# State-space stage: another order of the calls on all five engines, and a wait for the bank of the chunk summary

## The chip, the cores and the metric

The program runs on one core of one Trainium2 chip. The metric is device time in microseconds (us) of one execution. Five engines work side by side, each through its own list of instructions in order: TensorE (PE, matmuls and transposes), VectorE (DVE), ScalarE (ACT), GpSimd (POOL) and SyncE (SP, which here only issues DMAs). They meet through semaphores alone.

## The reference

Four layers follow one another over 4096 tokens of 256 channels. Only the first is touched, a chunked state-space layer (8 heads of 64, state 64, inner width 512):

```python
zxbcdt = u @ W_in.T;  z, xBC, dt = split(zxbcdt);  dt = softplus(dt + dt_bias)
xBC = silu(causal_conv4(xBC) + conv_b);  x, Bm, Cm = split(xBC)
xs = x * dt;  A_cum = cumsum(-exp(A_log) * dt)                  # within a chunk
Y_diag = einsum('bcln,bcsn,bchls,bcshp->bclhp', Cr, Br, L, xs)   # within a chunk
states = einsum('bchl,bcln,bclhp->bchpn', decay_states, Br, xs)  # summary of a chunk
Y_off  = Cr @ carried_state * exp(A_cum)                         # carried into a chunk
y = (Y_diag + Y_off + x * D) * silu(z)
y = y * rsqrt(mean(y * y) + eps) * norm_w
x = layernorm(u + y @ W_out.T)
```

The chunks are joined by a running state `S`: each chunk decays it and adds its own summary. A coupling network, a selective scan and a quantised feed-forward layer follow, and are not changed.

## The kernel before

`first_layer` works on NB = 8 blocks of 512 tokens (index `b`), each of NC = 4 chunks of 128 (index `j`; `g = 4b + j`). Each engine has one function (`sync`, `tensor`, `vector`, `scalar`, `pool`) with small local functions, called below *calls*, each a few instructions with the semaphore waits that they need. The order of the calls is written out by hand in a loop over `it`, in which an engine works on several blocks at once: `it`, `post = it - 1`, `last = it - 2`, `old = it - 3`. Nothing else sets the order.

The calls, by engine:
- TensorE. `project_dt(b)` and `project(b, i)`, i = 1 to 9, make the input projection (i = 1 to 5 go through the convolution, 6 to 9 are z), six matmuls each, into banks `b_p0` and `b_p1`. `prepare(b, j)` transposes a chunk into banks `b_bc` and `b_xt`, and for j = 0 the block's dt as well. `carried(b, j)` multiplies the spread state `Sb` with `CE`, `within(b, j)` adds the chunk's own part (`M`, `xs`), both into bank `b_y`. `summary(b, j)` makes the chunk's summary in bank `b_new`. `project_out(b, j)` multiplies with `W_out` into bank `b_op`. `turn_out(b, j)` transposes a finished chunk, also into `b_new`.
- VectorE. `conv(b, i)` (three taps), `decays(b, j)` (two scans into `L`), `mask` (`M` from `L`), `inputs` (`xs`), `state` (`S = Sd + b_new`), `gate` (`zs = b_y * zs`), `mean_square` (`ssn` from `b_op`), `residual` (`r` from `b_op`, then statistics), `ramps`, `soft_err`.
- ScalarE. `evac_conv(b, i)` (two passes over a bank), `silu_conv`, `silu_z`, `direct(b, j)` (x * D into `b_y`, four instructions), `spread_S(b, j)` (`S` into `Sb`, two instructions), `square`, `evac_B`, `normalize`, `evac_out`, and the softplus in pieces (`row_parts`, `row_exp`, `row_log`, ...).
- GpSimd. `ramped` (`CE`), `decayed` (`xd`), `state` (`Sd`), `squares`, `root` (`rms`), `low_u` (`ul`), `soft_fix`, `norm`, `add_tokens`.
- SyncE. `load_uT`, `store_rows` and `load_rows` (decay rows out to memory and back, spread over 128 partitions), `copy_C`, `load_u`.

Dependences that matter below: `carried(b, j)` needs `direct(b, j)`, `spread_S` of the chunk ahead and `CE`, and `within(b, j)` stands behind it; `gate(b, j)` needs `within(b, j)`; `direct(b, j + 1)` needs `gate(b, j)`, since both use `b_y`. `project_out(b, j)` needs the bank that `residual` of the chunk ahead reads, and `mean_square(b, j)` needs `project_out(b, j)`. `decays(b, j)` overwrites `L`, which `decayed` of the chunk ahead (GpSimd) reads. `prepare(b, 0)` needs all of a block's `silu_conv` and the copy `C2`.

Of the kernel before, what the change touches and what calls it, by code (L numbers as in the profile page):

```python
# [14 lines left out]
NB = T // TB  # L15
# [28 lines left out]
def build(nc, d, out, scratch):  # L44
    with ExitStack() as ctx:
# [46 lines left out]
        def first_layer():  # L92
# [74 lines left out]
            def sync(e):  # L167
# [42 lines left out]
                e.dma_start(W_dt[:, :, :], rows(d["W_dtT"])).then_inc(ld_Wd, DMAS)  # L210
                load_uT(0)
                load_W(0)
# [6 lines left out]
                copy_C(0)  # L219
                load_rows(0, 0)  # L220
                load_rows(0, 1)
                load_nets()
                for it in range(NB + 2):
                    last, post = it - 2, it - 1
                    if 0 < last < NB:
                        load_rows(last, 1)
                    if live(last):
                        load_rows(last, 2)
                    if 1 < it < NB:
                        load_uT(it)  # L230
                    if live(last):
                        load_rows(last, 3)
                        load_u(last)
                    if 0 < post < NB:
                        store_rows(post)
                        copy_C(post)
                        load_rows(post, 0)
# [3 lines left out]
            def tensor(e):  # L241
# [113 lines left out]
                project(0, 8)  # L355
                prepare(0, 0)
                project(0, 9)
                for it in range(NB + 3):
                    old, last, post = it - 3, it - 2, it - 1
                    if 0 < post < NB:  # L360
                        prepare(post, 0)
                    if live(old):
                        turn_out(old, 0)
                    if live(last):
                        project_out(last, 2)
                    if 0 < it < NB:
                        project_dt(it)
                        project(it, 1)
                    if live(post):
                        carried(post, 0)  # L370
                    if live(old):
                        turn_out(old, 1)
                    if 0 < it < NB:
                        project(it, 2)
                    if live(post):
                        within(post, 0)
                    if live(old):
                        turn_out(old, 2)
                    if live(post):
                        prepare(post, 1)  # L380
                    if live(old):
                        turn_out(old, 3)
                    if 0 < it < NB:
                        project(it, 3)
                    if live(post):
                        summary(post, 0)
                    if 0 < it < NB:
                        project(it, 4)
                    if live(last):
                        project_out(last, 3)  # L390
                    if live(post):
                        carried(post, 1)
                        summary(post, 1)
                        within(post, 1)
                        prepare(post, 2)
                    if 0 < it < NB:
                        project(it, 5)
                    if live(post):
                        project_out(post, 0)
                        carried(post, 2)  # L400
                    if 0 < it < NB:
                        project(it, 6)
                    if live(post):
                        within(post, 2)
                        summary(post, 2)
                        prepare(post, 3)
                    if 0 < it < NB:
                        project(it, 7)
                    if live(post):
                        project_out(post, 1)  # L410
                    if 0 < it < NB:
                        project(it, 8)
                        project(it, 9)
                    if live(post):
                        carried(post, 3)
                        summary(post, 3)
                        within(post, 3)

            def scalar(e):
# [109 lines left out]
                split_W(0)  # L529
                row_parts(0)  # L530
                row_exp(0)
                row_log(0)
                split_W(1)
                halo(0)
                row_decay(0)
                evac_conv(0, 0)
                split_W(2)
                evac_conv(0, 1)
                evac_conv(0, 2)
                silu_conv(0, 0)  # L540
                evac_conv(0, 3)
                evac_conv(0, 4)
                split_u(1)
                silu_conv(0, 1)
                silu_conv(0, 2)
                silu_conv(0, 3)
                silu_conv(0, 4)
                silu_z(0, 0)
                silu_z(0, 1)
                evac_B(0, 0)  # L550
                silu_z(0, 2)
                direct(0, 0)
                silu_z(0, 3)
                for it in range(NB + 3):
                    old, last, post = it - 3, it - 2, it - 1
# [4 lines left out]
                    if live(last):  # L560
                        direct(last, 2)
                        evac_B(last, 2)
                    if 0 < post < NB:
                        evac_conv(post, 4)
                    if live(last):
                        square(last, 1)
                    if 1 < it < NB:
                        split_u(it)
                    if 0 < post < NB:
                        silu_conv(post, 0)  # L570
                        silu_conv(post, 1)
                    if live(last):
                        evac_B(last, 3)
                    if 0 < post < NB:
                        silu_z(post, 0)
                    if live(last):
                        square(last, 2)
                    if 0 < post < NB:
                        silu_conv(post, 2)
                        silu_z(post, 1)  # L580
                        silu_conv(post, 3)
                    if live(last):
                        direct(last, 3)
                        spread_S(last, 2)
                    if 0 < post < NB:
                        silu_conv(post, 4)
                        silu_z(post, 2)
                    if 0 < it < NB:
                        halo(it)
                    if live(old):  # L590
                        normalize(old)
                    if 0 <= last < NB - 1:
                        spread_S(last, 3)
                    if 0 < post < NB:
                        evac_B(post, 0)
                        silu_z(post, 3)
                        direct(post, 0)
                    if live(old):
                        evac_out(old, 0)
                    if live(last):  # L600
                        square(last, 3)
                    if 0 < it < NB:
                        row_parts(it)
                        evac_conv(it, 0)
                    if live(old):
                        evac_out(old, 1)
                    if 0 < it < NB:
                        evac_conv(it, 1)
                    if live(old):
                        evac_out(old, 2)  # L610
                    if 0 < it < NB:
                        row_exp(it)
                    if live(old):
                        evac_out(old, 3)
                    if live(post):
                        evac_B(post, 1)
                    if 0 < it < NB:
                        evac_conv(it, 2)
                        row_log(it)
                    if live(post):  # L620
                        direct(post, 1)
                        spread_S(post, 0)
                    if 0 < it < NB:
                        evac_conv(it, 3)
# [2103 lines left out]
```

## Time and profile before

| what | us |
|---|---|
| time, median of 3 runs | 1157.51 (1157.15 to 1159.94) |
| span of the profiled execution | 1157.9 |
| state-space stage in it | 0 to about 334 |
| steady blocks in it, by the transpose of dt in `prepare(b, 0)` | 37.95 each |
| TensorE / VectorE / ScalarE / GpSimd busy, share of the span | 90 / 81 / 75 / 65 % |

The span is the time from the first to the last instruction of one profiled execution, and is 0.4 us above the median. No time of its own beyond that span is given for that execution, so sums below are made against the span and carried over to the median. A busy TensorE in this profile is not one at its peak: the ends of matmuls are modelled and overlap, so that its pace is read from the distance between starts.

### The profile page before, as it was taken

How to read it: one execution, taken by the hardware profiler on the slowest of the kernel's cores; microseconds unless marked ns; L12 is line 12 of the kernel's file. 1: busy time of each engine (PE TensorE's matmuls, PEld its weight loads, DVE VectorE, ACT ScalarE, POOL GpSimd, SP SyncE). 2: the span in 40 equal slices, each digit the busy share in tenths (PEclk: the TensorE clock that was granted, in tenths of full speed). 3: DMA queues.
4: the chain of work that ended last, by engine and by line, in shares of the span. 5: the costliest groups of instructions: out<-in, count | busy, mean ns of one | idle time of the engine just before them, and what ended most of it. 6: DMA issues, size and time to landing. Idle time of an engine off the chain costs nothing. (4 is left out here: it accounts for less than half of the span.)

```text
span 1157.9 us, 17435 instructions
## 1 busy us (share of the span) xinstructions
PE 1041.0 (90%) x5234; PEld 702.9 (61%) x5234; DVE 940.3 (81%) x1313; ACT 871.2 (75%) x1681; POOL 750.9 (65%) x644
## 2 busy tenths in 40 slices
PE   6999999999879999995758699999999999987987
PEld 4777777777633344444436467566676756656576
DVE  7999999999824665453999899999999999999741
ACT  7768878877534455557777899899998989996733
POOL 3466656675722453343687988989798997979320
PEclk9999999999979999997778899999999999999899
DMA  6444343433231011114766555456555555745301
GB/s 191 131 126 133 115 128 106 132 117 113 83 136 48 1 37 55 37 55 130 208 155 139 132 152 128 138 148 153 139 143 159 145 138 146 152 135 130 73 1 37
DMA packets 93232, 133.83 MB, mean 116 GB/s; under 512 B 8786, under 2 KB 47698, under 8 KB 93140
## 3 DMA queue, kind: packets, MB, share of 16 engines
q1 hardware_dynamic: 93140, 132.73, 41.9%
q8 instruction: 42, 0.69, 0.2%
q14 instruction: 50, 0.41, 0.1%
HBM read 116.45 MB, written 14.16 MB: 113 GB/s over the span
## 5 line engine op out<-in xcount | busy, mean ns | idle before, releaser
L2228 DVE TENSOR_TENSOR_SCAN state<-bank_a,h,state 128x512 f32<-128x512 f32 x256 | 316.7, 1270 | 28.4 <-POOL state L2498 11.8
L2498 POOL TENSOR_TENSOR state<-uc,Bb 128x1024 f32<-128x1024 f32 x64 | 150.8, 2368 | 34.4 <-DVE prod L2234 24.8
L2498 POOL TENSOR_TENSOR state<-s,Bb 128x1024 f32<-128x1024 f32 x64 | 150.6, 2367 | 29.6 <-DVE prod L2234 21.1
L1663 PE MATMUL bank_y<-ident,prod 128*128 128x128 f32 x1024 | 140.6, 285 | 29.5 <-DVE prod L2234 29.5
L1663 PEld LDWEIGHTS bank_y<-ident,prod 128*128 128x128 f32 x1024 | 124.9, 148 | 68.6 <-DVE prod L2234 37.0
L2234 DVE TENSOR_TENSOR prod<-state,bank_c 128x1024 f32<-128x1024 f32 x128 | 154.2, 1204 | 5.0 <-ACT bank_c L1884 2.8
L1708 PE MATMUL bank_m<-w,f_h 128*128 128x256 f32 x448 | 106.0, 387 | 0.0
L40 PE MATMUL bank_m<-nT,w 128*128 128x512 f32 x224 | 103.8, 601 | 0.9 <-ACT nT L1962 0.9
L1879 ACT ACTIVATE bank_a<-s,A 128x512 f32<-128x512 f32 x128 | 86.2, 680 | 12.2 <-DVE state L2228 12.1
L1879 ACT ACTIVATE bank_a<-dtc,A 128x512 f32<-128x512 f32 x128 | 86.4, 681 | 10.5 <-DVE state L2228 10.3
L1708 PEld LDWEIGHTS bank_m<-w,f_h 128*128 128x128 f32 x448 | 83.3, 192 | 15.8 <-issue 5.8
L1884 ACT ACTIVATE bank_c<-Cb 128x512 f32<-128x512 f32 x128 | 75.3, 588 | 15.9 <-DVE prod L2234 15.8
L879 POOL TENSOR_TENSOR xd<-xs,L 128x512 f32<-128x512 f32 x32 | 34.0, 1062 | 76.4 <-DVE xs L660 76.4
L671 DVE TENSOR_TENSOR_SCAN L<-abc,zeros,b_id 128x512 f32<-128x512 f32 x64 | 78.3, 1265 | 5.2 <-POOL xd L879 4.2
L1318 DVE TENSOR_SCALAR cS<-cS,slope,shift 128x512 f32<-128x512 f32 x24 | 13.1, 546 | 67.5 <-ACT cS L1230 67.5
L40 PEld LDWEIGHTS bank_m<-nT,w 128*128 128x128 f32 x224 | 40.8, 193 | 39.0 <-issue 37.4
L334 PE MATMUL b_op<-W_out,zs 128*128 128x256 f32 x256 | 63.5, 391 | 0.0
L638 DVE SCALAR_TENSOR_TENSOR b_p<-raw,columns,b_p 128x512 f32<-128x512 f32 x72 | 54.3, 754 | 3.8 <-ACT b_p L465 2.2
L40 PE MATMUL c<-h,nets 128*128 128x512 f32 x96 | 46.7, 609 | 3.7 <-ACT h L1211 3.6
L40 PE MATMUL b_p<-uh,W_h 128*128 128x512 f32 x132 | 47.9, 444 | 2.0 <-DVE W_l L716 1.7
L334 PEld LDWEIGHTS b_op<-W_out,zs 128*128 128x128 f32 x256 | 46.6, 192 | 5.0
L1968 ACT ACTIVATE f_h<-bank_m,columns 128x512 f32<-128x512 f32 x56 | 38.0, 679 | 6.7 <-PE bank_m L40 5.9
(387 smaller groups left out, 2553.0 us busy)
## 6 DMA issues: line engine op xcount, KB each, us to landing
Bb<-CB_rows SPq DMA_DIRECT2D x128, 256.0 KB, 4.1
Cb<-CB_rows SPq DMA_DIRECT2D x128, 256.0 KB, 4.7
abc<-decays SPq DMA_DIRECT2D x32, 512.0 KB, 4.5
Ebc<-ramps SPq DMA_DIRECT2D x64, 128.0 KB, 3.1
uT<-in_uT SPq DMA_DIRECT2D x8, 512.0 KB, 4.4
u<-in_u SPq DMA_DIRECT2D x8, 512.0 KB, 4.1
x_tokens<-x2s SPq DMA_DIRECT2D x8, 512.0 KB, 2.9
x_rows<-x1T SPq DMA_DIRECT2D x8, 512.0 KB, 2.7
```

Source lines behind the costliest of these rows:

```text
L40: i = e.matmul(out, w, x, start=(n == 0), stop=(n == len(pairs) - 1))
L334: i = e.matmul(b_op[:, 0:DM], zs[b % 2][:, m, ts], W_out[:, m, :], start=(m == 0), stop=(m == MD - 1))
L638: e.scalar_tensor_tensor(to, raw[:, m, t:t + TB], cw[:, m, t:t + 1], acc[:, :], ALU.mult, ALU.add).then_inc(v_conv, 1)
L671: e.tensor_tensor_scan(L[:, hs, :].rearrange("p h t -> p (h t)"), abc[g % 2][:, hs, :].rearrange("p h t -> p (h t)"), b_id[:, :], zeros[:, ...
L1663: i = e.matmul(p_y[c // 2][:, at:at + P], prod[n % 2][:, k, c * CH:(c + 1) * CH], ident[:, :], start=False, stop=(n == NS - 1), is_transpo ...
L1708: i = e.matmul(to, f_h[:, k, c * CH:(c + 1) * CH], w2[:, k, :], start=False, stop=(c % 2 == 1 and k == KF - 1))
L1879: e.activation(p_a[k][:, :], dtc[b % 2][:, k, :], ACT.Exp, scale=A[:, k, n:n + 1]).then_inc(a_a, 1)
L1884: e.activation(p_c[:, :], Cb[n % 4][:, :], ACT.Copy).then_inc(a_c, 1)
L1968: e.activation(f_h[:, m, :], pair[m % 2][:, :], ACT.Identity, bias=b1[:, m:m + 1]).then_inc(a_up, 1)
L2228: e.tensor_tensor_scan(s[:, k, :], p_a[k][:, :], s[:, k, :], h0[:, n, k:k + 1], ALU.mult, ALU.add).then_inc(v_s, 1)
L2234: e.tensor_tensor(prod[n % 2][:, :, :], state[(NS * b + n) % 3][:, :, :], both(p_c[:, :]), ALU.mult).then_inc(v_g, 1)
L2498: e.tensor_tensor(state[at % 3][:, :, :], uc[b % 2][:, :, :], both(Bb[n % 4][:, :]), ALU.mult).then_inc(p_b, 1)
```

## The change

All calls stay, with the same shapes and data. Their order is written anew on TensorE, ScalarE, VectorE and SyncE; on GpSimd only the first `low_u` moves, ahead of `scale_W_out`. One wait is added, in `summary`: `after(e, v_S, g)`, that is, `state` of the chunk ahead has read `b_new`. Before, `carried` of the same chunk, which waits for `spread_S` of the chunk ahead, stood ahead of `summary` and implied it.

```diff
@@ summary(b, j), TensorE
                     e.wait_ge(a_Bt, g + 1)
                     e.wait_ge(p_xd, g + 1)
+                    after(e, v_S, g)
                     after(e, a_tx, NC * (b - 1))
@@ SyncE, in the loop
                     if 0 < last < NB:
+                        store_rows(last)
+                        load_rows(last, 0)
                         load_rows(last, 1)
+                    if 1 < cur < NB:
+                        load_uT(cur)
                     if live(last):
                         load_rows(last, 2)
-                    if 1 < it < NB:
-                        load_uT(it)
-                    if live(last):
                         load_rows(last, 3)
                         load_u(last)
                     if 0 < post < NB:
-                        store_rows(post)
                         copy_C(post)
-                        load_rows(post, 0)
@@ TensorE, ahead of the loop
                 project(0, 8)
+                project(0, 9)
                 prepare(0, 0)
-                project(0, 9)
@@ TensorE, last part of the loop
+                    if 0 < cur < NB:
+                        project(cur, 7)
+                        project(cur, 8)
+                        project(cur, 9)
+                    if live(post):
+                        summary(post, 3)
+                    if 0 < cur < NB:
+                        prepare(cur, 0)
                     if live(post):
                         carried(post, 3)
-                        summary(post, 3)
+                    if 0 < nxt < NB:
+                        project_dt(nxt)
+                    if live(post):
                         within(post, 3)
+                    if live(last):
+                        turn_out(last, 0)
+                    if live(post):
+                        project_out(post, 2)
@@ VectorE, from the loop
                     if live(last):
-                        residual(last, 0)
+                        decays(last, 3)
+                        inputs(last, 3)
+                        state(last, 2)
                         gate(last, 2)
-                        decays(last, 3)
-                        state(last, 2)
-                        inputs(last, 3)
                         mean_square(last, 1)
@@ ScalarE, last part of the loop
                     if live(post):
                         square(post, 0)
+                    if 0 < cur < NB:
+                        row_plus_one(cur)
+                    if live(post):
+                        evac_B(post, 2)
+                        direct(post, 2)
```

On TensorE, at the end of a block's chunks (block 0's chunk 3, with projections of block 1), the order before was this; `b_y<-CE,Sb` is `carried`, `b_y<-M,xs` `within`, `b_new` `summary`, `b_bc` and `b_xt` `prepare` of the next block, `b_op` `project_out` of chunk 2, `b_p<-uT` `project_dt`.

```order
L301 MATMUL b_y<-CE,Sb 128x128 x4
L322 MATMUL b_new<-xd,Bt 64x256 x2
L310 MATMUL b_y<-M,xs 64x128 x8
L285 MATMUL b_bc<-ident,r_dt 128x128
L286 MATMUL b_bc<-ident,xf 128x128
L287 MATMUL b_bc<-C,xf 128x128
L291 MATMUL b_xt<-ident,xf 128x128 x4
L332 MATMUL b_op<-ones,sq 128x1
L334 MATMUL b_op<-W_out,zs 128x256 x4
L40 MATMUL b_p<-uT,W_dt 32x128 x8
```

And now:

```order
L322 MATMUL b_new<-xd,Bt 64x256 x2
L284 MATMUL b_bc<-ident,r_dt 128x128
L285 MATMUL b_bc<-ident,xf 128x128
L286 MATMUL b_bc<-C,xf 128x128
L290 MATMUL b_xt<-ident,xf 128x128 x4
L300 MATMUL b_y<-CE,Sb 128x128 x4
L40 MATMUL b_p<-uT,W_dt 32x128 x8
L309 MATMUL b_y<-M,xs 64x128 x8
L332 MATMUL b_op<-ones,sq 128x1
L334 MATMUL b_op<-W_out,zs 128x256 x4
```

`summary` and `prepare(b + 1, 0)` now stand ahead of `carried(b, 3)`, and `project_dt` ahead of `within(b, 3)`.

On VectorE, the stretch from the `gate` of chunk 2 to the `decays` of the next block (`zs` is `gate`, `L` `decays`, `S` `state`, `xs` `inputs`, `ssn` `mean_square`, `M` `mask`) was this:

```order
L694 TENSOR_TENSOR zs<-b_y,zs 128x4x128
L671 SCALAR_TENSOR_TENSOR L<-abc,zeros,b_id 128x512 x2
L687 TENSOR_TENSOR S<-Sd,b_new 128x256
L660 TENSOR_TENSOR xs<-b_xt,dtT 128x512
L700 TENSOR_SCALAR ssn<-b_op 128x1
L680 TENSOR_TENSOR M<-L,b_bc 128x1024
L671 SCALAR_TENSOR_TENSOR L<-abc,zeros,b_id 128x512 x2
```

And now:

```order
L673 SCALAR_TENSOR_TENSOR L<-abc,zeros,b_id 128x512 x2
L662 TENSOR_TENSOR xs<-b_xt,dtT 128x512
L689 TENSOR_TENSOR S<-Sd,b_new 128x256
L696 TENSOR_TENSOR zs<-b_y,zs 128x4x128
L702 TENSOR_SCALAR ssn<-b_op 128x1
L682 TENSOR_TENSOR M<-L,b_bc 128x1024
L673 SCALAR_TENSOR_TENSOR L<-abc,zeros,b_id 128x512 x2
```

The `gate` of chunk 2 has gone behind `decays`, `inputs` and `state`, and `inputs` ahead of `state`.

On ScalarE, from the `square` of chunk 0 on (`Sb` is `spread_S`, `b_y<-xf` `direct`, `r_da` `row_decay`, `Bt` `evac_B`), the order was this:

```order
L504 ACTIVATE sq<-zs 128x512
L488 ACTIVATE Sb<-S 64x4x64
L489 ACTIVATE Sb<-S 64x4x64
L453 ACTIVATE r_da<-r_dt,negA 128x128
L497 ACTIVATE b_y<-xf,columns 128x128 x4
L482 ACTIVATE Bt<-b_bc 128x64
```

And now:

```order
L505 ACTIVATE sq<-zs 128x512
L447 ACTIVATE r_vd<-r_va 128x128
L483 ACTIVATE Bt<-b_bc 128x64
L498 ACTIVATE b_y<-xf,columns 128x128 x4
L489 ACTIVATE Sb<-S 64x4x64
L490 ACTIVATE Sb<-S 64x4x64
L454 ACTIVATE r_da<-r_dt,negA 128x128
```

`direct` of chunk 2 now stands ahead of `spread_S` of chunk 1, instead of behind it.

## Rows read from the trace of the kernel before

**Rows 1.** Busy time of each engine in one period: us, then PE, PEld, DVE, ACT, POOL, PEclk, DMA
```profile
137.90:175.87 37.97, 37.85 (x262) 29.45 (x261) 36.05 (x60) 30.95 (x71) 25.61 (x33) 1.00 0.40 122
```

**Rows 2.** Waits of VectorE, 45 to 290 us: total, times, longest
```profile
DVE L L671 <- POOL xd L879: 4.0, 6, 0.7
```

**Rows 3.** Timeline of VectorE in one period: start, length, instruction
```profile
133.49 0.69 DVE L660 TENSOR_TENSOR xs<-b_xt,dtT 128x512 f32<-128x512 f32 x1
...
141.70 0.15 DVE L700 TENSOR_SCALAR ssn<-b_op 128x1 f32<-128x1 f32 x1
...
142.52 2.45 DVE L671 TENSOR_TENSOR_SCAN L<-abc,zeros,b_id 128x512 f32<-128x512 f32 x2 [0.68 <-POOL xd L879]
...
158.06 0.41 DVE L687 TENSOR_TENSOR S<-Sd,b_new 128x256 f32<-128x256 f32 x1
...
159.57 0.69 DVE L694 TENSOR_TENSOR zs<-b_y,zs 128x512 f32<-128x512 f32 x1
```

**Rows 4.** Timeline of GpSimd in the same period
```profile
141.36 1.07 POOL L879 TENSOR_TENSOR xd<-xs,L 128x512 f32<-128x512 f32 x1
```

**Rows 5.** Timeline of TensorE over one period
```profile
137.85 0.33 PE L285 MATMUL b_bc<-ident,r_dt 128*128 128x128 f32 x1
...
141.99 0.73 PE L40 MATMUL b_p<-uh,W_h 128*128 128x512 f32 x2
...
156.93 0.33 PE L286 MATMUL b_bc<-ident,xf 128*128 128x128 f32 x1
...
158.02 0.71 PE L40 MATMUL b_p<-uh,W_h 128*128 128x512 f32 x2
...
161.59 1.16 PE L301 MATMUL b_y<-CE,Sb 128*128 128x128 f32 x8
...
162.56 0.73 PE L40 MATMUL b_p<-uh,W_h 128*128 128x512 f32 x2
...
164.28 1.09 PE L310 MATMUL b_y<-M,xs 128*64 128x128 f32 x16
...
165.74 0.33 PE L286 MATMUL b_bc<-ident,xf 128*128 128x128 f32 x1
...
167.12 0.72 PE L40 MATMUL b_p<-uh,W_h 128*128 128x512 f32 x2
...
171.95 0.63 PE L40 MATMUL b_p<-uh,W_h 128*128 128x512 f32 x2
...
173.36 1.05 PE L301 MATMUL b_y<-CE,Sb 128*128 128x128 f32 x8
...
175.80 0.33 PE L285 MATMUL b_bc<-ident,r_dt 128*128 128x128 f32 x1
```

**Rows 6.** Timeline of ScalarE, in a period and in the tail
```profile
138.72 0.41 ACT L489 ACTIVATE Sb<-S 64x256 f32<-64x256 f32 x1
...
160.30 1.25 ACT L497 ACTIVATE b_y<-xf,columns 128x128 f32<-128x128 f32 x4 [0.41 <-DVE zs L694]
...
300.54 0.41 ACT L489 ACTIVATE Sb<-S 64x256 f32<-64x256 f32 x1
...
311.58 1.23 ACT L497 ACTIVATE b_y<-xf,columns 128x128 f32<-128x128 f32 x4
```

**Rows 7.** Timeline of TensorE at the start and in the tail
```profile
25.83 0.69 PE L291 MATMUL b_xt<-ident,xf 128*128 128x128 f32 x4 [3.25 <-ACT xf L469]
...
26.25 1.14 PE L40 MATMUL b_op<-uh,W_h 128*128 128x512 f32 x2
...
301.20 1.13 PE L301 MATMUL b_y<-CE,Sb 128*128 128x128 f32 x8 [0.53 <-ACT Sb L489]
...
314.90 1.13 PE L301 MATMUL b_y<-CE,Sb 128*128 128x128 f32 x8 [1.86 <-POOL CE L870]
```

**Rows 8.** Timeline of VectorE at the start and in the tail
```profile
33.04 1.54 DVE L638 SCALAR_TENSOR_TENSOR b_p<-raw,columns,b_p 128x512 f32<-128x512 f32 x2 [1.21 <-ACT b_p L465]
...
310.32 0.69 DVE L694 TENSOR_TENSOR zs<-b_y,zs 128x512 f32<-128x512 f32 x1
```

More of the change, by code:

```diff
@@ L392, in tensor @@
                         carried(post, 1)
-                        summary(post, 1)
                         within(post, 1)
-                        prepare(post, 2)
-                    if 0 < it < NB:
-                        project(it, 5)
+                        project_out(post, 0)
+                    if 0 < cur < NB:
+                        project(cur, 5)
                     if live(post):
-                        project_out(post, 0)
                         carried(post, 2)
-                    if 0 < it < NB:
-                        project(it, 6)
+                        summary(post, 2)
@@ L403, in tensor @@
+                    if 0 < cur < NB:
+                        project(cur, 6)
                     if live(post):
+                        prepare(post, 3)
                         within(post, 2)
[L405 to L408, printed above, removed]
+                        project_out(post, 1)
+                    if 0 < cur < NB:
+                        project(cur, 7)
+                        project(cur, 8)
+                        project(cur, 9)
@@ L576, in scalar @@
[L576 to L589, printed above, removed]
@@ L590, in scalar @@
                     if live(old):
                         normalize(old)
+                    if 1 < cur < NB:
+                        split_u(cur)
+                    if 0 < post < NB:
+                        silu_z(post, 1)
+                        silu_conv(post, 4)
+                    if live(last):
+                        spread_S(last, 2)
+                        square(last, 2)
+                        direct(last, 3)
+                    if 0 < post < NB:
+                        evac_B(post, 0)
+                        silu_z(post, 2)
@@ L613, in scalar @@
+                    if 0 < cur < NB:
+                        evac_conv(cur, 1)
+                        silu_conv(cur, 0)
                     if live(old):
                         evac_out(old, 3)
[L615 to L619, printed above, removed]
+                    if 0 < cur < NB:
+                        row_exp(cur)
+                        evac_conv(cur, 2)
@@ L765, in vector @@
                 for it in range(NB + 2):
-                    last, post = it - 2, it - 1
+                    last, post, cur = it - 2, it - 1, it
+                    if live(last):
+                        state(last, 1)
+                        inputs(last, 2)
                     if 0 < post < NB:
@@ L788, in vector @@
                         residual(last, 1)
+                    if live(post):
+                        inputs(post, 0)
+                    if live(last):
                         gate(last, 3)
                     if live(post):
-                        inputs(post, 0)
                         mask(post, 0)
```

152 lines of the change are left out of this document (70 added, 82 removed).

## Prediction

> **What bounds the kernel now.** I read the windows of single periods first, then the waits of VectorE, then the timelines of the engines side by side. In a steady block TensorE and VectorE both count as full: 37.85 and 36.05 us busy of 37.97, at the full clock (PEclk 1.00), where ScalarE has 30.95 and GpSimd 25.61 [rows 1]. The busy sum of TensorE flatters it, since ends overlap, so VectorE's waits decide. They are all of one kind: six times 0.6 to 0.7 us, 4.0 us together, `decays` for `xd` on GpSimd [rows 2]. One period from one dt transpose to the next is 175.80 - 137.85 = 37.95 us [rows 5]; without its wait of 0.68 [rows 3] VectorE would need 37.27. That is the floor of any order, and six periods at it would give back 4.0 us, or 0.35%. The rest of what an order can change lies at the two ends: 1.21 us for which VectorE waits for the first `evac_conv` of block 1 [rows 8], and the tail behind the last block, where TensorE waits 1.86 us for `CE` [rows 7]. Everything from about 334 us on runs the same instructions. A measurement of this kernel tells from no change what is beyond about 0.3%, 3.5 us.
>
> **Part 1, the wait that goes.** Before, `inputs(b, 3)` starts on VectorE at 133.49, the `decays` that waits at 142.52: 9.03 us, of which 0.68 waiting, so 8.35 of work [rows 3]. GpSimd fills these 9.03 us with a chain that starts from this `inputs` and ends with `decayed(b + 1, 0)`, 141.36 + 1.07 = 142.43 [rows 4], 0.09 ahead of the `decays`. Now `state(b, 2)` and `gate(b, 2)` stand between the two on VectorE: 0.41 and 0.69 long [rows 3], less some 0.1 by which each overlaps the next, 0.9 together. VectorE reaches `decays` after 8.35 + 0.9 = 9.25, behind GpSimd's 9.03. GpSimd's order is unchanged there, so this wait goes, with 0.2 us to spare: worth 0.68 a period by itself.
>
> **Part 2, the wait that may come instead.** `project_out(b, 2)` moved to the end of TensorE's iteration, behind `summary(b, 3)`, `prepare(b + 1, 0)`, `carried(b, 3)`, `project_dt` and `within(b, 3)`, and `mean_square(b, 2)`, which reads it, stands right ahead of the `decays` of part 1. And ScalarE now does `direct(b, 2)` ahead of `spread_S(b, 1)`. That closes a loop through three engines, which I price once round:
> - VectorE from `mean_square(b, 2)` to `gate(b + 1, 1)`: 159.57 - 141.70 = 17.87, less the wait 0.68, less `state(b + 1, 1)`, which now comes after the gate, 0.32: 16.87 [rows 3].
> - gate start to `direct` start: 160.30 - 159.57 = 0.73; `direct` itself 1.25; `spread_S` behind it, two times 0.41, 0.82 [rows 3, 6].
> - `spread_S` end (300.54 + 0.41 = 300.95) to `carried` start (301.20): 0.25 [rows 6, 7].
> - TensorE from `carried(b, 2)` to the end of `project_out(b, 2)`. The same 16 calls stand in the trace in two pieces, 161.59 to 175.80 (14.21) and 137.85 to 141.99 (4.14), 18.35 together [rows 5]. Two calls in it hold waits: `project(b, 6)` takes 164.28 - 162.56 = 1.72 where `project(b, 9)` takes 173.36 - 171.95 = 1.41, and `prepare(b, 3)` takes 167.12 - 165.74 = 1.38 where `prepare(b, 2)` takes 158.02 - 156.93 = 1.09 [rows 5]. Less 0.31 and 0.29: 17.75.
> - the last matmul's end to `mean_square`, 0.1 as an estimate from releases in the trace (a gate that ends at 160.26 and the `direct` at 160.30).
>
> Sum: 16.87 + 0.73 + 1.25 + 0.82 + 0.25 + 17.75 + 0.10 = 37.77 us a round. A round is a period, so the period can't fall to 37.27; the wait of 0.68 turns into one of about 0.5 at `mean_square(b, 2)`, for TensorE. Gain 37.95 - 37.77 = 0.18, in six periods 1.1 us. The uncertain term is TensorE's 17.75. Where calls meet in other pairs, loads of weights are hidden better or worse. Bounds: not less than VectorE's floor (gain 4.0), and, if each of the four projections in it takes the 1.72 of the slowest in the period and nothing is subtracted for `prepare`, 17.75 + 4 x 0.31 + 0.29 = 19.28, 39.3 a round, a loss of 8.1. I take 37.77, since these are the durations of the same calls, with only the two clear waits taken out.
>
> **Part 3, the other moves.** The wait for `v_S` in `summary(b, 1)` costs nothing: `state(b, 0)` is now followed on VectorE by `mean_square(b - 1, 3)` and `conv(b + 1, 2)`, and TensorE has `project_out(b - 1, 3)` and `project(b + 1, 4)` ahead of this `summary`. Were that cover gone, `prepare(b, 2)`, `carried(b, 1)` and `within(b, 1)` would queue behind it and `gate(b, 1)` would wait for them; `carried(b, 1)` needs `spread_S` of the same `state` anyhow, so that at most the `summary` and `prepare` in front of it, about 1.6 us, would move into the path. `silu_conv(b, 0)` early on ScalarE, ahead of the exponential, adds no table load, as the z activations ahead of it use the same table; it waits for `conv(b, 0)`, and `evac_conv(b, 2)` behind it is wanted by VectorE only after `inputs`, `conv(b, 1)`, `gate`, `mask` and `state`. On SyncE `copy_C` is ahead of `store_rows` and `load_uT(b + 2)` ahead of `load_rows(b, 2)`; the only releaser of VectorE's waits in steady blocks is `xd`, never a DMA [rows 2], and each of these moves by one or two calls of a few us a period at most, so nothing for them.
>
> **Part 4, the start.** Two opposite things. `project(0, 9)` is now ahead of `prepare(0, 0)`. Before, TensorE idled 3.25 us in the middle of `prepare(0, 0)` and then ran that projection at the lower level of its clock, two matmuls in 1.14 us where 0.72 is usual [rows 5, 7]. Now it is out of the way of `project_dt(1)`, and VectorE's 1.21 us before `conv(1, 0)` [rows 8] shrink. Against this, uT(0) is loaded behind W(0), the first weights are split only after the logarithm, and `silu_conv(0, 0)`, from which `C2` is copied, comes behind `evac_conv(0, 4)`, so `prepare(0, 0)` starts later. Bounds: the whole 1.21 gained, or about 1 lost, by the projection (1.4) and split (1.05) that moved. I take 0.5 gained. By the Trainium skill, "TensorE: Matmul & The Clock Gate", What's actually happening, the array's default is the throttled state, and only activity releases it; the slow projection behind the gap agrees. By that rule the gap now meets `prepare(0, 0)` and `project_dt(1)` instead, half a microsecond of the gain would go, and the sum would end at 1156.7.
>
> **Part 5, the tail.** In the last block `gate(7, 2)`, before at 310.32 [rows 8], comes behind `decays`, `inputs` and `state`, 2.45 + 0.69 + 0.41 less overlaps, 3.3 us later [rows 3]; its `residual` ahead comes about 0.6 earlier, because `mask` now covers the root. So the gate is near 313.0, ScalarE squares (0.6) and then does `direct(7, 3)` (1.23 [rows 6]), and `carried(7, 3)` starts near 315.6 instead of 314.90 [rows 7]; but `summary(7, 3)`, 0.5, is no longer between it and `within(7, 3)`. Net 0.2 to 0.4 lost; I take 0.1 more for the round of part 2 that the last periods carry in, less what `mean_square(6, 3)` gives back, and put 0.3 lost in all (bounds 0.5 gained, 1.0 lost).
>
> **Sum.** -1.1 - 0.5 + 0.3 = -1.3 us on a span of 1157.9, which is 0.4 above the median of 1157.51: 1156.6 for the span, 1156.2 for the median.
>
> **Rivals.**
> - The loop is quicker than priced and VectorE runs at its floor. For it: TensorE's calls overlap in places, and part 1's slack is real. Against it: the 16 calls are priced from the trace, and 17.75 would have to be 17.25. Gain 4.0 + 1.2 at the start - 0.2: 1152.5. It counts as faster from a round below 37.5 together with 0.5 to 1 at the start. Chance 0.28.
> - The loop is slower, TensorE becoming the bound, since `direct(b, 2)` ahead of `spread_S(b, 1)` holds `carried(b, 2)` in every block. For it: a projection can take 1.72. Against: VectorE's mask ends just there. It decides from 37.95 + 3.7 / 6 = 38.6 a round; at 38.7 the loss is 4.5, less 0.2 at the ends: 1161.8. Chance 0.10.
> - The start or the tail misses by more than its bounds while the periods stay as forecast: 1154 to 1159, either side. Chance 0.05.
> - The forecast, a wait traded for a shorter one: 1156.2, by itself 1154.2 to 1158.3. Chance 0.57.
>
> The range leaves out the far part of the first two rivals: 1152.0 to 1160.5. Faster gets the first and half of the third rounded down, 0.30; slower the second and the rest, 0.13; same 0.57.
>
> **What would show it.** Right: the wait of `decays` for `xd` is gone from VectorE's list, and one of `mean_square`'s lines for `b_op` of about 0.5 us stands in its place, six or seven times; dt transposes 37.8 apart; `conv(1, 0)` near 32.5; the last `gate` about 0.3 later relative to the last period. Wrong: dt transposes 37.3 apart (first rival), or 38.6 and more with waits of TensorE for `Sb` (second); waits of VectorE with a DMA or ScalarE's `b_p` as releaser, which part 3 excludes, would break the argument itself.

## The result, and the profile after

| | before | changed |
|---|---|---|
| median, us | 1157.94 (1157.15 to 1160.08, 6 runs) | 1162.2 (1161.11 to 1163.79, 6 runs) |
| span of the profiled execution | 1157.9 | 1162.0 |
| last transpose of the stage (`x1T`) on ScalarE | 333.48 | 337.64 |
| one steady period | 37.95 | 38.95 |

The ratio is 1.0033, 95% interval 1.0022 to 1.0045: slower by 4.3 us, where 1.3 us faster was forecast, and 1.7 us above the range. All of it arises in the first layer, whose last `x1T` is 4.16 later.

To find the stretch, I take `soft_err`, which VectorE does once a block. From block 1 to block 7 it starts at 44.83 and 271.75 before, at 44.68 and 276.27 now. So the start gives 0.15, the six periods between take 4.67 more (231.59 for 226.92), and from there to the last `x1T` it is 61.37 for 61.73, 0.36 less: 4.16. The period is the whole question. Behind the last `x1T` every kernel runs the same instructions, and the profiled executions of this document take between 822.7 and 826.6 us for them. A difference of 1 or 2 us between the times of two kernels can thus lie there, and what an edit does to the loop is read from the period.

Windows of the changed kernel, one period (columns as in [rows 1]):

```profile
137.64:176.59 38.95, 38.27 (x262) 29.22 (x260) 36.80 (x59) 30.61 (x71) 25.57 (x33) 1.00 0.42 119
```

VectorE is busy 0.75 us more than in [rows 1] with the same calls, and TensorE 0.42, both at the full clock (1.00). What VectorE waits for, 45 to 290 us (total, times, longest):

```profile
DVE ssn L702 <- PE b_op L334: 2.8, 6, 0.5
DVE zs L696 <- PE b_y L309: 2.2, 6, 0.5
```

and TensorE in the same stretch:

```profile
PE b_y L300 <- ACT Sb L490: 3.5, 6, 0.6
PE b_p L40 <- DVE xf L640: 0.2, 1, 0.2
```

The wait for `xd` of [rows 2] is gone, and `mean_square` waits for `b_op` in its place, six times about half a microsecond: both as forecast. Besides, `gate` waits for `b_y`, and TensorE waits for `Sb`. Now the round of part 2, on VectorE:

```profile
143.96 0.16 DVE L702 TENSOR_SCALAR ssn<-b_op 128x1 f32<-128x1 f32 x1 [0.49 <-PE b_op L334]
...
159.43 0.78 DVE L644 SCALAR_TENSOR_TENSOR r_vd<-r_vd,r_va 128x128 f32<-128x128 f32 x1
...
161.31 0.69 DVE L696 TENSOR_TENSOR zs<-b_y,zs 128x512 f32<-128x512 f32 x1
```

on ScalarE:

```profile
156.14 0.60 ACT L464 ACTIVATE raw<-b_p 128x512 f32<-128x512 f32 x1 [1.19 <-PE b_p L40]
156.77 0.75 ACT L466 ACTIVATE b_p<-b_p,columns 128x512 f32<-128x512 f32 x1
157.45 0.40 ACT L489 ACTIVATE Sb<-S 64x256 f32<-64x256 f32 x1
157.86 0.41 ACT L490 ACTIVATE Sb<-S 64x256 f32<-64x256 f32 x1
...
158.52 0.61 ACT L505 ACTIVATE sq<-zs 128x512 f32<-128x512 f32 x1
...
162.03 1.25 ACT L498 ACTIVATE b_y<-xf,columns 128x128 f32<-128x128 f32 x4 [2.60 <-DVE zs L696]
163.22 0.40 ACT L489 ACTIVATE Sb<-S 64x256 f32<-64x256 f32 x1
163.63 0.42 ACT L490 ACTIVATE Sb<-S 64x256 f32<-64x256 f32 x1
```

on TensorE, to the end of `project_out(b, 2)`:

```profile
158.53 1.13 PE L300 MATMUL b_y<-CE,Sb 128*128 128x128 f32 x8 [0.58 <-ACT Sb L490]
...
164.31 1.13 PE L300 MATMUL b_y<-CE,Sb 128*128 128x128 f32 x8
165.37 0.65 PE L322 MATMUL b_new<-xd,Bt 128*64 128x256 f32 x4
165.95 0.73 PE L40 MATMUL b_p<-uh,W_h 128*128 128x512 f32 x2
...
167.44 0.27 PE L285 MATMUL b_bc<-ident,xf 128*128 128x128 f32 x1
...
168.65 1.09 PE L309 MATMUL b_y<-M,xs 128*64 128x128 f32 x16
...
180.75 0.28 PE L332 MATMUL b_op<-ones,sq 128*128 128x1 f32 x2
...
182.70 0.38 PE L344 MATMUL b_new<-ident,r 128*128 128x128 f32 x2
```

and on GpSimd, beside VectorE's 159.43:

```profile
159.33 0.72 POOL L901 TENSOR_TENSOR sq<-sq 128x256 f32<-128x256 f32 x1 [3.09 <-ACT sq L505]
```

The round closes exactly: `mean_square` to `gate` 161.31 - 143.96 = 17.35 (forecast 16.87), to `direct` 0.72 (0.73), to `carried` 164.31 - 162.03 = 2.28 (2.32), and `carried` to the next `mean_square`, 182.90, 18.59 (17.85): 38.94, the period to within the rounding of the rows. Two of its terms are off, by 0.48 and 0.74.

The 0.48 is `soft_err`. It took 0.27 before and takes 0.78 now in blocks 3 to 7 (0.47 in block 2), between operations that are as long as they were. It starts 0.10 after GpSimd's `squares`, which ends at 160.05, and ends at 160.21. `squares` is late because ScalarE's `square(b, 0)`, at 158.52, stands behind `evac_conv(b + 1, 3)`, which waited 1.19 for TensorE. By the Trainium skill, "SBUF — State Buffer", "SBUF: two separate sides", a VectorE operation with two operands in SBUF and a GpSimd one that reads SBUF hold a shared port by an exclusive lock, and the second waits for the end of the first. The trace agrees: both of `soft_err`'s operands are in SBUF, and its end follows GpSimd's, whatever its start. In block 2 it is this pair:

```profile
81.85 0.47 DVE L644 SCALAR_TENSOR_TENSOR r_vd<-r_vd,r_va 128x128 f32<-128x128 f32 x1
```

```profile
81.44 0.73 POOL L901 TENSOR_TENSOR sq<-sq 128x256 f32<-128x256 f32 x1 [2.84 <-ACT sq L505]
```

It starts 0.41 behind `squares` there instead of 0.10, takes 0.47 instead of 0.78, and ends 0.15 behind it (82.32 and 82.17), as in the steady blocks (160.21 and 160.05).

The 0.74: from `carried(b, 2)` to the start of `turn_out` behind `project_out(b, 2)` it is 182.70 - 164.31 = 18.39. The like stretch of before is 17.75 (the 18.35 less 0.60 taken out as waits), so 0.64 is TensorE's, and `mean_square` comes 0.20 behind that point instead of the estimated 0.1. No wait stands in the stretch. The 0.64 is spread over the joints: from start to start, `summary` takes 165.95 - 165.37 = 0.58 where the two of before took 165.74 - 165.21 = 0.53 and 0.48, `carried` 1.06 where it took 0.97 and 0.98, `within` 1.02 for 0.93, `prepare` 1.21 where I took 1.09. One of these was to be read before: the trace of the kernel before has a `summary` with a projection behind it, as here, and it takes 150.78 - 150.20 = 0.58:

```profile
150.20 0.65 PE L322 MATMUL b_new<-xd,Bt 128*64 128x256 f32 x4
150.78 0.74 PE L40 MATMUL b_p<-uh,W_h 128*128 128x512 f32 x2
```

And the 1.06 of `carried(b, 2)` is not a joint: between the same neighbours it takes 0.98 in experiments 1, 2 and 10, where `Sb` is there in time, and 1.06 here and in experiment 9, where it is released by `Sb`. So 0.08 of the 0.64 comes with the loop itself, and 0.56 with the neighbours.

### The profile page after: what moved, and what is told of

The parts are those of the page before. It is cut to its first block and busy times, and to the rows that moved or that the text cites. A ratio compares the mean times of both kernels' runs of the same rounds, so it can differ in the third digit from the quotient of the medians.

```text
span 1162.0 us, 17459 instructions
## 1 busy us (share of the span) xinstructions
PE 1046.4 (90%) x5234; PEld 703.8 (61%) x5234; DVE 944.9 (81%) x1313; ACT 868.9 (75%) x1681; POOL 750.3 (65%) x644
## 5 line engine op out<-in xcount | busy, mean ns | idle before, releaser
L1671 PEld LDWEIGHTS bank_y<-ident,prod 128*128 128x128 f32 x1024 | 128.7, 151 | 67.0 <-DVE prod L2242 35.3
L1671 PE MATMUL bank_y<-ident,prod 128*128 128x128 f32 x1024 | 144.4, 290 | 26.9 <-DVE prod L2242 26.9
L498 ACT ACTIVATE b_y<-xf,columns 128x128 f32<-128x128 f32 x128 | 39.5, 356 | 22.4 <-DVE zs L696 22.4
```

The source lines that it names most:

```text
L498: i = e.activation(b_y[:, m * CH:(m + 1) * CH], xf[b % 2][:, m, j * CH:(j + 1) * CH], ACT.Copy, scale=Dcol[:, m:m + 1])
L1671: i = e.matmul(p_y[c // 2][:, at:at + P], prod[n % 2][:, k, c * CH:(c + 1) * CH], ident[:, :], start=False, stop=(n == NS - 1), is_transpo ...
```

## The experiments

I had two theories. First, `soft_err` costs the period its 0.5, by way of GpSimd. Second, the order has several loops through TensorE that are nearly as long as each other, so that shortening one gains only as far as the next: B, the one that I priced; C, `project(b + 1, 4)` to `evac_conv(b + 1, 3)` to `spread_S(b, 0)` to `carried(b, 1)`; A, `residual(b - 1, 3)` to `project_out(b, 0)`, which share a bank. The rivals were the added wait, and a loop B that is slow by itself through `direct` ahead of `spread_S`. In what follows a period is the distance of two `soft_err` in the steady blocks.

**1. The square early.** ScalarE's `square(b, 0)` moves ahead of `evac_conv(b + 1, 3)`.

```diff
                     if live(post):
                         direct(post, 1)
+                        square(post, 0)
                     if 0 < cur < NB:
                         evac_conv(cur, 3)
...
-                    if live(post):
-                        square(post, 0)
```

> The changed kernel, with ScalarE's square(b, 0) moved ahead of evac_conv(b + 1, 3), so that GpSimd's squares(b, 0) is over before VectorE's soft_err. Theory (a loop through VectorE, ScalarE and TensorE sets the period of 38.95 us, and soft_err takes 0.78 us instead of 0.27 inside it because GpSimd's squares runs beside it): soft_err back to 0.27, dt transposes 38.45 apart, 6 x 0.5 = 3.0 us less, 1159.2. Rival 1 (TensorE's own calls are the bound, its waits apart): it waits about 0.8 us a period in the changed kernel, so soft_err may shorten and the period falls to 38.45 too. Rival 2 (soft_err is long for another reason, such as ScalarE's write just ahead): still 0.78, no change of time, 1162.2.

1163.19 us, ratio 1.0043 (1.0029 to 1.0057), period 38.65. VectorE and GpSimd in the same place:

```profile
159.47 0.27 DVE L643 SCALAR_TENSOR_TENSOR r_vd<-r_vd,r_va 128x128 f32<-128x128 f32 x1
```

```profile
156.25 0.72 POOL L900 TENSOR_TENSOR sq<-sq 128x256 f32<-128x256 f32 x1
```

With `squares` over at 156.97, `soft_err` is back at 0.27: its length follows GpSimd's time, not the changed order as such. The period fell by 0.30, not 0.5, and TensorE's wait for `Sb` stayed at 3.5 in six: another loop took over. The distances from start to start show what went, since the list leaves out TensorE's shortest waits. In the changed kernel `within(b, 1)` takes 1.19 to the start of `project_out(b, 0)`, which waits for `r` (loop A), and `project(b + 1, 5)` 1.66 to `carried(b, 2)`, which waits for `Sb` (loop B); here it is 1.02 and 1.58, and `carried(b, 2)` itself takes 0.98 for 1.06. These 0.17, 0.08 and 0.08 account for the 0.30 to within 0.03, and what still waits is `carried(b, 1)`, loop C. The times of the two kernels can't be told apart: this one's last `x1T` is 1.15 earlier, and it loses that again behind the stage (both spans are 1162.0).

**2. `spread_S` first.** Loop B opened: `spread_S(b, 1)` ahead of `direct(b, 2)` on ScalarE, with `state(b, 1)` ahead of `residual(b - 1, 3)` on VectorE.

```diff
@@ ScalarE
+                    if live(last):
+                        direct(last, 2)
                     if 0 < post < NB:
                         evac_conv(post, 4)
...
                         evac_B(post, 2)
-                        direct(post, 2)
@@ VectorE
                     if live(last):
-                        state(last, 1)
                         inputs(last, 2)
...
                         soft_err(cur)
+                    if live(post):
+                        state(post, 1)
                     if live(last):
                         residual(last, 3)
```

> The changed kernel, with spread_S(b, 1) ahead of direct(b, 2) on ScalarE and state(b, 1) ahead of residual on VectorE, as in the kernel before; all else as changed. Theory (the loop): spread_S (0.82 us and 0.25 to TensorE) leaves the loop, 0.05 and state's 0.31 come in: 38.95 - 0.7 = 38.25 us a period, 1162.2 - 4.0 = 1158.2. Rival 1 (TensorE's own calls are the bound): the period stays at or above 38.1 to 38.9, its waits of 0.8 being all that can go. Rival 3 (the loss is in the wait for v_S in summary): nothing changes, 1162.2.

1166.28 us, ratio 1.0069 (1.0048 to 1.0090), period 39.08: longer. TensorE's waits show why:

```profile
PE b_y L300 <- ACT Sb L490: 3.5, 6, 0.6
PE b_op L332 <- DVE r L711: 2.4, 6, 0.4
```

`residual(b - 1, 3)` is later by the `state` ahead of it, and `project_out(b, 0)` waits for it: loop A has taken B's place. So undoing `direct` ahead of `spread_S` gains nothing here. Since `spread_S(b, 1)` needs `state(b, 1)`, this edit opens B only by putting the `state` into A, so that it doesn't price B alone.

**3. Both of these**, the edits of 1 and 2 together.

> Both edits of the two runs ahead. Theory (the loop): 38.95 - 0.5 - 0.7 = 37.75 us a period, 7.2 us less, 1155.0. Rival 1 (TensorE's own calls are the bound, some 38.1 us without waits): 38.1 a period, 5.1 us less, 1157.1, and TensorE never waits. Rival 3 (v_S): nothing, 1162.2.

1163.09 us, ratio 1.0045 (1.0026 to 1.0065), period 38.65, as with the square alone.

**4. `summary` back.** TensorE's `summary(b, 1)` goes behind `carried(b, 1)` again, where the added wait can't cost.

```diff
                     if live(post):
-                        summary(post, 1)
                         prepare(post, 2)
                         carried(post, 1)
+                        summary(post, 1)
                         within(post, 1)
```

> The changed kernel, with summary(b, 1) behind carried(b, 1) and prepare(b, 2), where the wait for v_S is already met. Theory: no part of the loop, and the wait for v_S is covered in all blocks but the first: within 0.5 us of 1162.2. Rival 3 (the wait for v_S and the place of this summary cost the time): some 4 us less, 1158.

1166.46 us, ratio 1.0075 (1.0052 to 1.0098), period 39.09. TensorE:

```profile
PE b_y L300 <- ACT Sb L490: 7.9, 6, 1.3
```

`summary` had filled part of the time that `carried(b, 1)` waits for `Sb`, and without it the wait is 1.3 instead of 0.6 each. The place of `summary` helps. Nor does the added wait hold it: in the changed kernel `state(b, 0)` ends at 154.82 and `summary(b, 1)`, which needs it, starts at 156.03, and the other three chunks have more room.

**5. The added wait alone.** The kernel before, with the wait in `summary` and nothing else.

```diff
                     e.wait_ge(p_xd, g + 1)
+                    after(e, v_S, g)
```

> Before, with the added wait of summary for state of the chunk ahead and nothing else. Theory: carried of the same chunk stands ahead and has waited for spread_S of that state, so the wait is met when summary reaches it: period 37.95, ratio 1.000, 1157.9. Rival: a further wait on TensorE costs some tens of ns at each of 32 summaries, 1 us or more.

1158.03 us, ratio 0.9998 (0.9989 to 1.0006), period 37.95. It costs nothing there, where `carried` ahead of it implies it anyhow; for the new order the rows of experiment 4 speak.

**6. TensorE's new order alone, and 7. VectorE's new order alone**, each in the loop of the kernel before, with the added wait. These show whether one engine's order carries the loss.

The edits are the part of the change's diff for that engine; here the end of TensorE's, and the middle of VectorE's.

```diff
@@ 6, TensorE
                         summary(post, 3)
+                    if 0 < cur < NB:
+                        prepare(cur, 0)
+                    if live(post):
+                        carried(post, 3)
@@ 7, VectorE
+                        decays(last, 3)
+                        inputs(last, 3)
+                        state(last, 2)
                         gate(last, 2)
```

> The kernel before, with only TensorE's loop in the changed order (and the wait for v_S that this order needs). Theory (three loops of nearly the same length all run through TensorE, whose new order costs about 0.6 us more a period at the seams between calls): soft_err a period apart at 38.3 to 38.7 us, 1160 to 1162. Rival 4 (TensorE's order is harmless, the loss is ScalarE's and VectorE's new order): 37.95, 1157.7.

> The kernel before, with only VectorE's loop in the changed order (the wait for v_S is in it too, and always met). Theory: the wait of decays for xd (0.68 us) goes, and TensorE in its old order has 0.6 us of slack, so that the period falls to between 37.3 and 37.7 us, 1154 to 1156.5. Rival 4: ScalarE, still in the old order, waits for gate(b, 2), which now comes 3.3 us later, and holds direct, spread_S and TensorE: 38.3 and more, 1160.

TensorE's: 1171.35 us, ratio 1.0113 (1.0092 to 1.0134), period 39.75. VectorE's: 1197.51 us, 1.0331 (1.0312 to 1.0350), period 43.34. Both are worse than all together, so that the loss isn't a sum of parts by engine, and neither run says which edit costs what.

**8. All three loops moved.** On ScalarE `square(b, 0)` and `spread_S(b, 0)` ahead of `evac_conv(b + 1, 3)`, and `spread_S(b, 1)` ahead of `direct(b, 2)`. On VectorE `state(b, 1)` between `residual(b - 1, 3)` and `gate(b, 1)`, and:

```diff
-                    if live(last):
-                        mean_square(last, 2)
                     if live(post):
                         decays(post, 1)
                     if live(last):
-                        residual(last, 2)
+                        mean_square(last, 2)
                     if 0 < cur < NB:
                         conv(cur, 0)
+                    if live(last):
+                        residual(last, 2)
```

> The changed kernel with its three loops opened and TensorE's order untouched: square(b, 0) early, spread_S(b, 0) ahead of evac_conv(b + 1, 3), spread_S(b, 1) ahead of direct(b, 2), state(b, 1) between residual and gate, mean_square(b, 2) behind decays and its residual behind conv. Theory: what is left is TensorE's own need in this order, 38.95 less its waits of 0.8 and 0.1: 38.0 us a period, 1162.2 - 5.7 = 1156.5, and TensorE without waits. Rival 1b (another loop of about 38.6 remains, as in the two runs with the early square): 38.6, 1160 to 1163.

1166.69 us, ratio 1.0071 (1.0052 to 1.0091), period 39.21, against the expectation. TensorE, then VectorE:

```profile
PE b_op L332 <- DVE r L710: 7.3, 6, 1.4
```

```profile
DVE b_p L641 <- ACT b_p L466: 5.7, 6, 1.0
```

With `residual` moved, `conv(b + 1, 0)` stands first and waits 0.95 a block for `evac_conv`: the `residual` had hidden that. The wait for `Sb` is gone. Of the 39.21, TensorE waits 1.2 by its list, so that its own work takes 38.0 at most (experiment 10 has it closer).

**9. Loop C opened alone.** On top of experiment 1, `spread_S(b, 0)` goes ahead of `evac_conv(b + 1, 3)` as well.

```diff
                         square(post, 0)
-                    if 0 < cur < NB:
-                        evac_conv(cur, 3)
                     if live(post):
                         spread_S(post, 0)
                     if 0 < cur < NB:
+                        evac_conv(cur, 3)
```

> After, with two of ScalarE's calls moved: square of chunk 0 and spread_S of chunk 0 both ahead of evac_conv(b + 1, 3) (the first of them alone gave a period of 38.65 us with soft_err back at 0.27). Theory: three loops through TensorE are nearly equal, and the one that holds the period at 38.65 is project(b + 1, 4) -> evac_conv(b + 1, 3) -> spread_S(b, 0) -> carried(b, 1). This edit opens that one, so TensorE's wait for Sb at carried(b, 1) (3.5 us in six) goes, and the next loop decides: the one of my prediction, 38.95 less 0.5 for soft_err = 38.45 a period. Six periods at 38.45 against 37.95 lose 3.0, less 0.5 at the ends: about 1160.4. Rival: the loop of project_out(b + 1, 0) behind residual(b, 3) holds it; then the wait for Sb becomes one for residual and the period stays at 38.65, 1161.5 or more. Second rival: TensorE's own need decides, 38.0, about 1158.

1161.17 us, ratio 1.0022 (1.0013 to 1.0032), period 38.46 (six took 229.39): 38.45 was expected. The wait for `Sb` is gone, one for `r` of 2.6 in six stands in its place, and the round of part 2 reads, on VectorE,

```profile
143.49 0.16 DVE L701 TENSOR_SCALAR ssn<-b_op 128x1 f32<-128x1 f32 x1 [0.49 <-PE b_op L334]
...
160.34 0.69 DVE L695 TENSOR_TENSOR zs<-b_y,zs 128x512 f32<-128x512 f32 x1
```

160.34 - 143.49 = 16.85, against 16.87 forecast, so that what is left of the error is TensorE's. This has the shortest period of the kernels made from the changed one. Its interval lies below that of experiment 2 and all the way above 1, but overlaps those of the changed kernel and of experiments 1, 3 and 10.

**10. Loops B and C opened.** Experiments 2 and 9 together.

> The kernel with both of ScalarE's calls moved, and spread_S of chunk 1 ahead of direct of chunk 2 with state(b, 1) ahead of residual(b - 1, 3) on VectorE besides. It opens my prediction's loop (direct(b, 2) no longer ahead of spread_S(b, 1)) as well as the one through evac_conv(b + 1, 3). Theory: what remains is the loop through residual(b - 1, 3) and project_out(b, 0), 16.17 + 0.33 on VectorE and TensorE's stretch, 39.1 with soft_err at 0.78 and so 38.6 without, 0.5 below the 39.08 of the kernel that had soft_err slow; TensorE waits for r. 1161. Rival: nothing but TensorE's own need of 38.0 is left, 1158.

1162.8 us, ratio 1.0037 (1.0023 to 1.0052), period 38.58, with one wait of TensorE in every block left:

```profile
PE b_op L332 <- DVE r L710: 4.5, 6, 1.0
```

That is loop A, as expected, 0.50 below experiment 2: the price of `soft_err` again, now in a kernel where it counts in full. Taken together, C holds the period at 38.65, A (with `state` in it) at 38.58, B at 38.46. TensorE's own work is less than all three, and the starts tell it:

```profile
158.53 1.09 PE L309 MATMUL b_y<-M,xs 128*64 128x128 f32 x16
160.33 0.35 PE L332 MATMUL b_op<-ones,sq 128*128 128x1 f32 x2 [0.70 <-DVE r L710]
```

From `within(b, 1)` to `project_out(b, 0)` it is 1.80, where it is 1.02 in experiment 1, which has no wait there: 0.78 waited, and 38.58 - 0.78 = 37.80. The changed kernel and experiment 9, with their longer lists of such differences, give 37.80 and 37.79. So with every loop opened the new order of TensorE could gain 0.15 a period on the 37.95 of before at best, and the old order runs at 37.60 in experiment 12.

**11. The start undone.** The changed kernel, with what stands ahead of the loop as it was before, on all five engines; of it TensorE's:

```diff
                 project(0, 8)
-                project(0, 9)
                 prepare(0, 0)
+                project(0, 9)
```

> After, with what stands ahead of the loop put back to its order of before on all five engines (project(0, 9) behind prepare(0, 0) again). Theory: the start was worth 0.15 us of span (soft_err of block 1 0.15 earlier), so that this kernel is 0.1 to 0.3 slower than the changed one or the same: period 38.95 unchanged, ratio to before 1.003 to 1.004. Rival, the half microsecond of my prediction: 0.5 us slower than the changed one in soft_err of block 0 and 1 alike.

1164.31 us, ratio 1.0046 (1.0033 to 1.0058), period 38.95. `soft_err` of block 1 is at 45.95, 1.27 later than in the changed kernel. But with the same start before has it at 44.83, the kernel of experiment 5 at 45.92 and that of experiment 12, whose one swap comes later, at 43.60, so that one profile of each can't settle 1 or 2 us here, and the ratios overlap. In both late executions TensorE's clock stays at its lower level (1.2 of 2.4 GHz) longer. Windows of experiment 5's kernel, of which the last but two is the granted clock:

```profile
28.00:30.00 2.00, 2.00 (x16) 1.25 (x18) 1.80 (x3) 1.03 (x3) 1.80 (x3) 0.50 1.15 300
30.00:32.00 2.00, 2.00 (x16) 1.38 (x9) 1.80 (x2) 0.84 (x4) 1.07 (x1) 0.56 0.43 141
```

Before has 0.57 and 1.00 in these two windows, behind the gap of 3.25 us of [rows 7], and the kernel of experiment 5 a gap of 3.78. The kernel of experiment 12, with the earliest `soft_err`, has 1.00 in both, behind 2.90. The changed kernel, behind one of 2.02 us that ends at 26.38, has 0.50 and 0.79. What the start is worth is less than this scatter of 2.3 us and stays open, its sign too.

**12. `inputs` ahead of `state`, in the kernel before.** One swap of the change taken alone, to test part 1.

```diff
                         decays(last, 3)
-                        state(last, 2)
                         inputs(last, 3)
+                        state(last, 2)
                         mean_square(last, 1)
```

> The kernel before, with inputs(b, 3) ahead of state(b, 2) on VectorE and nothing else. Theory: GpSimd's chain starts 0.31 us earlier, the wait of decays for xd falls from 0.68 to 0.37, the period from 37.95 to 37.65: 1.9 us less, 1155.8. Rival 5 (TensorE is as much the bound as VectorE): no change, 1157.7.

1157.61 us, ratio 0.9988 (0.9976 to 1.0000), period 37.60 instead of 37.95. VectorE:

```profile
DVE L L671 <- POOL xd L879: 1.7, 5, 0.3
```

The wait falls from 0.68 to 0.34 in a steady block, the period by 0.35. In the time it is not told from no change: its interval ends at 1.0000.

## Why the prediction was wrong

- *What bounds the kernel, and part 1: right.* Before, the wait for `xd` sets the period; it went in the changed kernel, and experiment 12 turned 0.35 of it into 0.35 a period. But it was worth 0.68 at most, and the new order costs TensorE nearly as much (0.56 at the joints).
- *Part 2, the loop: right in its form, wrong in two terms, and it decided the result.* The round is there, `mean_square` waits the half microsecond, and the sum of the measured terms is the period. "TensorE from `carried(b, 2)` to the end of `project_out(b, 2)`", 17.75, is 18.39, and the 0.1 behind it 0.20: I took the pace of calls from their neighbours in the old order, and in the new one nine of the sixteen take 0.04 to 0.12 more, one 0.09 less. In eight of the nine the neighbours are what differs; the ninth, `carried(b, 2)`, is released late. For `summary` ahead of a projection, 0.58 against the 0.53 that I took, the trace of before had the right number. The text said that the joints could differ and gave bounds, then took the middle as if the error were small. "VectorE from `mean_square(b, 2)` to `gate(b + 1, 1)`", 16.87, is 17.35: it assumed that the operations keep their length when an operation of GpSimd moves beside them. Experiments 1 and 9 give it back at 16.85. The errors of 0.48 and 0.74 together with 0.05 the other way make 37.77 into 38.94. The first two of the six periods, before the round is closed, lost 0.40 and 0.31 and the other four 1.0 each: 4.67 lost, where 1.1 gained was forecast.
- *What part 2 left out.* It priced one loop. With `soft_err` repaired two others stand within 0.2 us of it (experiments 9 and 10), and C decides, at 38.65. All three are above the 37.95 of before, so that no repair of one of them would have made the forecast true.
- *Part 3: right.* The added wait costs nothing before (experiment 5) and is met 1.21 us early in the changed kernel; experiment 4 shows `summary(b, 1)` in its new place as a help of 0.14 a period. No DMA came up as a releaser in the steady blocks.
- *Part 4, the start, and part 5, the tail: not told apart from scatter.* Forecast 0.5 gained and 0.3 lost, profiled 0.15 and 0.36 gained; `conv(1, 0)` was to be near 32.5 and is at 32.94. With an unchanged start this `conv` is anywhere from 31.88 to 34.13 and the first `soft_err` from 43.60 to 45.92 (experiments 12 and 5), so that the 0.5 can be neither confirmed nor refuted. TensorE's clock does fall behind the new, shorter gap as well (0.50 from 28 to 30 us), but what that costs isn't told apart either. From the last `soft_err` to `x1T` it takes 61.73, 60.65 and 62.19 in before and the kernels of experiments 5 and 12, which end as before but for one swap, so 0.36 means nothing either. Neither decides the result.
- *The rivals.* The second, TensorE slower from 38.6 a round, is what came, with 1161.8 as its price for 38.7. At 38.95 in all six it would be 1163.3; with the 4.67 that the six lost it is 1162.0, and 1162.2 was measured. Its sign came true in part: TensorE does wait for `Sb`, but most of it at `carried(b, 1)`. Its stated ground, `direct(b, 2)` ahead of `spread_S(b, 1)`, gave nothing when it was undone (experiments 2 and 10); the joints and `soft_err` made the period long. A chance of 0.10 was too little for a term whose bounds went from 37.3 to 39.3 a round around a break-even at 37.95.

## What to carry over

When an order written by hand gives a wait away, price every loop that the new order closes, not only the one in sight: here three ended within 0.2 us of each other, and repairing one moved the period to the next. Take the pace of TensorE's calls with the neighbours that they will have: look in the whole trace for the same call with the same call behind it. Where it doesn't show the pair, put 0.05 to 0.1 us on each new joint before calling a margin of 0.2 a gain. And look at what runs on GpSimd beside each VectorE operation with two operands in SBUF, since a delay on ScalarE alone can bring them together.

## What the runs showed of the hardware

- A VectorE operation of 0.27 us with both operands in SBUF took 0.78 when it started 0.10 behind a GpSimd operation on SBUF, 0.47 when it started 0.41 behind it, and 0.27 again when that one was 3 us earlier. In the first two cases it ended 0.16 and 0.15 behind GpSimd's end. The operations with an operand in PSUM around it did not change in length.
- The same calls on TensorE, without a wait, take 0.04 to 0.12 us more or less with the call that follows (`summary` 0.48 ahead of `within`, 0.53 ahead of `prepare`, 0.58 ahead of a projection). `carried` takes 0.98 between the same neighbours, and 1.06 when `Sb` comes late. What makes the difference at each joint these runs don't show.
- Steady periods of one order repeat to 0.1 us over executions (six of them 226.92 and 226.89; 231.59 and 231.69), while the first 45 us of one order differ by 2.3 us (43.60, 44.83, 45.92), and the longer TensorE's clock stays at its lower level behind the gap, the later they end (0.50 and 0.56 in the two windows from 28 to 32 us of the latest, 1.00 and 1.00 of the earliest).
